# A retention layer's attention core in plain fp32, with the values stationary in four 32-column groups

## The reference

```python
x = L0_attn_x                                  # (4, 1024, 256), fp32
xn = _layernorm(x, axis=-1)
x = x + attn(xn, ...) + ffn(xn, ...)

# attn: 16 heads of 16 channels, no softmax
q, k, v = (xn @ W.T).reshape(b, t, 16, 16)     # W_q, W_k, W_v
decay = where(i >= j, gammas[h] ** (i - j), 0)
attn = einsum('bihd,bjhd->bhij', q, k) * decay / sqrt(16)
y = einsum('bhij,bjhd->bihd', attn, v)
yn = (y - mean) / sqrt(var + EPS)              # over time and channels of each head
out = (yn * gn_weight + gn_bias) @ W_o.T

# ffn: the best 2 of 8 experts for each token
h = relu(xn @ w1[e] + b1[e]);  y_e = h @ w2[e] + b2[e]
out = sum over the two experts of softmax gate * y_e
```

## Time and profile before

| | us |
|---|---|
| median of 3 runs | 861.91 (861.26 to 863.84) |
| the profiled execution | 863.81 |
| its span, first to last instruction | 862.0 |
| TensorE busy in it | 811.3 (94%) |
| VectorE busy | 675.8 (78%) |
| ScalarE busy | 605.8 (70%) |
| GpSimd busy | 416.1 (48%) |

### The profile page before, as it was taken

How to read it: one execution, slowest core, us unless ns; L and a number is a source line. 1 busy time by engine, 2 the same in 40 slices (tenths; PEclk the granted TensorE clock), 3 DMA queues, 4 the chain that set the end, 5 groups by cost and what they waited for, 6 DMA issues and landing times.

```text
span 862.0 us, 21824 instructions
## 1 busy us (share of the span) xinstructions
PE 811.3 (94%) x6976; PEld 775.1 (90%) x6976; DVE 675.8 (78%) x1187; ACT 605.8 (70%) x1073; POOL 416.1 (48%) x352
## 2 busy tenths in 40 slices
PE   3947999999999999989999999999999999999967
PEld 1436999999999999989999999999999999999967
DVE  6687888888888889878778787787877878778646
ACT  2825575767666666767887778877788777887690
POOL 2107777777777677043444434444434443344320
PEclk9977999999999999999999999999999999999998
DMA  9984222222222223758888888878888888888239
GB/s 289 364 308 123 75 82 74 80 73 80 68 82 71 78 71 136 272 182 210 213 244 237 249 220 218 229 236 248 232 202 233 238 246 223 212 238 235 47 76 333
DMA packets 89050, 157.89 MB, mean 183 GB/s; under 512 B 26496, under 2 KB 66560, under 8 KB 78976
## 3 DMA queue, kind: packets, MB, share of 16 engines
q1 hardware_dynamic: 74720, 138.87, 49.1%
q0 software_dynamic: 14304, 18.69, 13.5%
HBM read 111.67 MB, written 37.37 MB: 173 GB/s over the span
## 4 chain that ended last, share of the span: by engine, by line
PE 87%; DVE 5%; issue 3%; DMA 2%; ACT 1%; SPq 1%; POOL 0%; POOLq 0%; DVEq 0%; ACTq 0%
PE ps L662 27%; PE ps L869 26%; PE ps L780 12%; PE ps L718 5%; PE ps L752 3%; PE ps L728 2%; PE ps L926 2%; PE ps L854 2%; PE ps L737 2%; PE ps L680 1%; PE ps L767 1%; DMA xn<-x 1%; PE ps L709 1%; PE ps L804 1%; PE ps L672 1%
## 5 line engine op out<-in xcount | busy, mean ns | idle before, releaser
L662 PE MATMUL ps<-arena_r 128*128 128x256 f32 (+1 forms) x2064 | 262.1, 284 | 0.4 <-ACT xn L561 0.4
L662 PEld LDWEIGHTS ps<-arena_r 128*128 128x128 f32 x2064 | 250.6, 191 | 4.8 <-issue 0.6
L869 PE MATMUL ps<-arena_r 128*128 128x256 f32 x1872 | 232.7, 284 | 0.8 <-DVE gn_t L1287 0.8
L869 PEld LDWEIGHTS ps<-arena_r 128*128 128x128 f32 x1872 | 228.9, 193 | 0.9 <-issue 0.9
L452 POOL TENSOR_TENSOR fence_out<-eps_col 128x1 f32<-128x1 f32 x39 | 78.8, 2020 | 260.3 <-DVE arena_f L1217 260.3
L507 ACT ACTIVATE arena_r<-arena_f 128x2048 fp32r<-128x2048 f32 x78 | 145.5, 1921 | 0.0
L454 POOL DMA_INDIRECT sum_rows<-arena_f,pair_slot x78 | 123.8, 1588 | 18.1 <-issue 17.2
L595 ACT ACTIVATE arena_f<-ps,arena_f 128x256 f32<-128x256 f32 x156 | 65.4, 473 | 90.4 <-PE ps L869 77.8
L780 PE MATMUL ps<-arena_r 128*128 128x128 f32 x1024 | 120.5, 276 | 0.0
L780 PEld LDWEIGHTS ps<-arena_r 128*128 128x128 f32 x1024 | 116.9, 192 | 0.0
L1233 DVE TENSOR_TENSOR arena_r<-arena_f,arena_r 128x2048 fp32r<-128x2048 f32 x39 | 89.4, 2292 | 34.8 <-ACT arena_r L507 34.8
(11 more groups left out here) (143 smaller groups left out, 1103.5 us busy)
## 6 DMA issues: line engine op xcount, KB each, us to landing
arena_f<-w SPq DMA_DIRECT2D x78, 1024.0 KB, 6.1
xs_rows<-spare_rows SPq DMA_DIRECT2D x39, 258.0 KB, 3.7
arena_f<-xs_rows SPq DMA_DIRECT2D x39, 258.0 KB, 3.9
pair_chunk<-xn SPq DMA_DIRECT2D x32, 256.0 KB, 2.5
arena_f<-b SPq DMA_DIRECT2D x39, 128.0 KB, 4.0
xn<-x SPq DMA_DIRECT2D x8, 512.0 KB, 8.9
x_chunk<-xn SPq DMA_DIRECT2D x32, 128.0 KB, 2.0
arena_f<-sum_rows SPq DMA_DIRECT2D x8, 512.0 KB, 7.5
```

Of the source, the lines that this page charges most:

```text
L662: last = pe.matmul(out_ap, lhs(a), rhs(b), start=start and n == 0, stop=stop and n == 2, **kw)
L869: last = pe.matmul(ps[:, 2 + hp, o * SLOT:(o + 1) * SLOT], w1_r[par][:, a, at:at + P], xs_r[:, b, k * SLOT:(k + 1) * SLOT], start=(m == 0 ...
```

## The change

The attention core (scores, state sums, across, inside) drops the split. Scores, keys, queries, values and state stay plain fp32 and go to the matmuls as they are. With that go the high and low parts on ScalarE, VectorE and GpSimd. In `inside` the operands change sides: a head's values (padded to 32 columns with zeros, `v_pad`) are stationary in one of four column groups, and the masked scores stream. The output lies with channels on partitions, so the y transposes and `output_sum` go. Each matmul of `across` has the state stationary and the queries stream, into the same layout. Keys and queries are transposed in separate steps to banks 6 and 5. The scores of a chunk are now issued at the end of the step before. The buffers are placed anew, so that the weights of slot 0 can be loaded ahead of the wait for the scatters; slot 1's wait for the last `inside`.

```diff
-            run_steps(pool, -2, NT, 4, 28, step)
+            run_steps(pool, 0, NT, 4, 28, chunk_scatter)
...
+            sp.wait_ge(s["route_done"], 1)
+            weights_load(0, 0)
+            for par in range(2):
+
+                sp.wait_ge(s[f"scat{par}"], 16 * NT)
+            rows_load(0, 0)
             bias_load(0, 0)
 
-            sp.wait_ge(s["s_l_pool"], NB // 2 * NT)
-            sp.wait_ge(s["s_l_dve"], NB // 2 * NT)
-            slot_load(1, 1)
+            sp.wait_ge(s["y_psum"], NT)
+            weights_load(1, 1)
+            rows_load(1, 1)
...
+            def diagonal_queries(n, par):
+                act.wait_ge(s["qt_psum"], n + 1)
+
+                wait(act, s["s_psum"], NB * (n - 1))
+                for o in range(QH):
+                    nc.scalar.activation(q_diag[:, par, :, o * P:(o + 1) * P], ps[:, 5, D:2 * D].rearrange("p (c i) -> p c i", c=KC),
+                                         ACT.Copy, scale=C["own_head"][:, o:o + 1]).then_inc(s["q_diag"], 1)
...
             def chunk(i, par):
+                if within(i - 1, NT):
+                    output_back(i - 1, 1 - par)
                 if within(i, NT):
+                    queries_back(i, par)
+                if within(i + 1, NT):
+                    values(i + 1, 1 - par)
+                if within(i + 1, NT):
+                    keys_back(i + 1, 1 - par)
+                if within(i + 1, NT):
+                    diagonal_queries(i + 1, 1 - par)
                 if within(i + 2, NT):
+                    tokens_high(i + 2, par)
...
+            run_steps(act, 0, NT, 4, 28, chunk)
+            w_high(0, 0, 0)
+            w_high(1, 0, 0)
+            chunk(NT, NT % 2)
...
             def scores(n, par):
...
                 for c in range(KC):
+                    for g in range(NB):
+                        rows = slice(g * QR, (g + 1) * QR)
...
+                        last = pe.matmul(ps[:, g, c * QH * P:(c + 1) * QH * P], kq_t[rows, par, 0, c * P:(c + 1) * P],
+                                         q_diag[rows, par, c], start=True, stop=True)
...
+            def across(n, par):
...
+                for c in range(KC):
+                    last = pe.matmul(ps[:, 7, c * P:(c + 1) * P], state_f[:, c], kq_t[:, par, 1, c * P:(c + 1) * P],
+                                     start=(c == 0), stop=False, skip_group_check=True)
...
+            def inside(n, par):
...
+                for c in range(KC):
+                    for o in range(QH):
                         for g in range(NB):
+                            h = c * HP + g * QH + o
+                            last = pe.matmul(ps[g * QR:(g + 1) * QR, 7, c * P:(c + 1) * P], v_pad[:, par, h * 2 * DH:(h + 1) * 2 * DH],
+                                             s_f[:, g, (c * QH + o) * P:(c * QH + o + 1) * P], start=False,
+                                             stop=(c == KC - 1 and o == QH - 1), skip_group_check=True)
...
+            def state_sums(n, par):
...
+                    last = pe.matmul(ps[:, 6, 256 + c * P:256 + (c + 1) * P], kq_f[:, par, c * P:(c + 1) * P], v_own(par, c),
+                                     start=(c == 0), stop=(c == KC - 1), skip_group_check=True)
...
             def chunk(i, par):
+                if within(i + 1, NT):
+                    query_projection(i + 1, 1 - par)
+                if within(i + 1, NT):
+                    key_transposes(i + 1, 1 - par)
                 if within(i, NT):
+                    across(i, par)
                 if within(i + 2, NT):
                     x_transposes(i + 2, par)
+                if within(i + 1, NT):
+                    query_transposes(i + 1, 1 - par)
+                if within(i, NT - 1):
+                    state_sums(i, par)
+                if isinstance(i, int) and i == NT - 1:
+                    pe.wait_ge(s["s_f"], NT * NB)
+                    slot_transposes(0, 0)
+                if within(i, NT):
+                    inside(i, par)
+                if within(i + 1, NT):
+                    scores(i + 1, 1 - par)
                 if within(i + 2, NT):
                     key_value_projection(i + 2, par)
...
             def chunk(i, par):
+                if within(i - 2, NT):
+                    output_stats(i - 2)
+                if within(i - 1, NT - 1):
+                    state_sum(i - 1)
+                if within(i + 1, NT):
+                    tokens_low(i + 1, 1 - par)
+                if within(i - 1, NT - 1):
+                    new_state(i - 1)
                 if within(i, NT):
                     masked_scores(i, 0)
                 if within(i, NT):
                     masked_scores(i, 1)
+                if within(i + 1, NT):
+                    keys(i + 1, 1 - par)
                 if within(i, NT):
                     masked_scores(i, 2)
                 if within(i + 1, NT):
+                    queries(i + 1, 1 - par)
                 if within(i, NT):
                     masked_scores(i, 3)
...
+            chunk(NT, NT % 2)
+            chunk(NT + 1, 1 - NT % 2)
             w1_low(0, 0)
             xs_low(0, 0)
```

More of the change, by code:

```diff
@@ L194, in build @@
         rse = ff(NS, E)
+        after_route = ff.at
         ff.at = 0
@@ L705, in x_transposes @@
                 pe.wait_ge(s[f"xc{par}"], (n - par) * 8 + 16)
-                wait(pe, s["v_f"], n)
+                wait(pe, s["v"], n)
                 for k in range(KC):
@@ L730, in query_projection, with slot_transposes @@
                 last.then_inc(s["q_psum"], 1)
-            def kq_transposes(n, par):
-                pe.wait_ge(s["k_f"], n + 1)
+            def slot_transposes(sl, par):
+                pe.wait_ge(s[f"xs_in{par}"], (sl - par) * 8 + 16)
+                wait(pe, s["xst_h"], sl - 1)
+                wait(pe, s["xst_l"], sl - 1)
+                for k in range(KC):
+                    for j in range(SJ):
+                        last = pe.transpose(ps[:, par, (k * SJ + j) * P:(k * SJ + j + 1) * P], xs[:, par, j, k * P:(k + 1) * P], ident)
+                last.then_inc(s["xst_psum"], 1)
@@ L735, in kq_transposes, with key_transposes, query_transposes @@
+            def key_transposes(n, par):
+                pe.wait_ge(s["k_f"], n + 1)
+                wait(pe, s["st_t"], n - 1)
+                for c in range(KC):
+                    last = pe.transpose(ps[:, 6, c * P:(c + 1) * P], kq_f[:, par, c * P:(c + 1) * P], ident)
+                last.then_inc(s["kt_psum"], 1)
+            def query_transposes(n, par):
                 pe.wait_ge(s["q_f"], n + 1)
-                for c in range(2 * KC):
-                    last = pe.transpose(ps[:, 5, c * P:(c + 1) * P], kq_f[:, par, c * P:(c + 1) * P], ident)
@@ L738, in kq_transposes @@
-                last.then_inc(s["kqt_psum"], 1)
+                for c in range(KC):
+                    last = pe.transpose(ps[:, 5, (KC + c) * P:(KC + c + 1) * P], kq_f[:, par, (KC + c) * P:(KC + c + 1) * P], ident)
+                last.then_inc(s["qt_psum"], 1)
             def scores(n, par):
-                pe.wait_ge(s["kqt_h"], n + 1)
-                pe.wait_ge(s["kqt_l"], n + 1)
+                pe.wait_ge(s["k_t"], n + 1)
                 pe.wait_ge(s["q_diag"], QH * (n + 1))
                 for c in range(KC):
-                    for m, (a, b) in enumerate(PASSES):
-                        for g in range(NB):
-                            rows = slice(g * QR, (g + 1) * QR)
-                            if c == 0 and m == 0:
-                                wait(pe, s["s_f"], NB * (n - 1) + g + 1 if not isinstance(n, int) or n > 0 else 0)
-                            last = pe.matmul(ps[:, g, c * QH * P:(c + 1) * QH * P], kq_t[rows, par, 0, a, c * P:(c + 1) * P],
-                                             q_diag[rows, par, b, c], start=(m == 0), stop=(m == 2))
-                            if c == KC - 1 and m == 2:
-                                last.then_inc(s["s_psum"], 1)
@@ L770, in across @@
                 last.then_inc(s["across_done"], 1)
             def inside(n, par):
-                pe.wait_ge(s["s_h"], NB * (n + 1))
-                pe.wait_ge(s["s_l_pool"], 2 * (n + 1))
-                pe.wait_ge(s["s_l_dve"], 2 * (n + 1))
-                for h in range(H):
-                    g, col = h % HP // QH, (h // HP * QH + h % QH) * P
-                    for a in range(2):
-                        last = pe.matmul(ps[:, 7, h // HB * P:(h // HB + 1) * P],
-                                         s_r[:, par, a, g, col:col + P],
-                                         v_wide[:, par, h // HB, h % HB * P:(h % HB + 1) * P], start=False,
-                                         stop=(h == H - 1 and a == 1), skip_group_check=True)
+                pe.wait_ge(s["s_f"], NB * (n + 1))
@@ L837, in _ @@
             for k in range(2):
-                last = pe.matmul(ps[:, 6 + k, 0:NT * E], token_sets[:, k], mask_bf[:], start=True, stop=True)
```

(17 more changed lines are left out.)

297 lines of the change are left out of this document (80 added, 217 removed).

## The result

The changed kernel takes 774.5 us (median), the kernel before 862.9 beside it: a ratio of 0.897, 95% interval 0.894 to 0.900. The profiled execution took 773.2 us with a span of 771.4.

What follows compares the result with a forecast made beforehand. TensorE was taken to bound the attention stage, its chunk falling from 8.66 to 7.5 us: 35 us over 29 periods, plus 3 at the start and 1 at the end, 39 off 861.9, gives 823 us; range 792 to 878.

Steps and rivals of the forecast that it cites:

- The terms that stay: TensorE's chunk work kept: projections and x transposes at 2.29 us, key and query transposes at 0.46.
- The three changes of form: TensorE switching between whole array and row or column groups, three times a chunk at 0.1 us each.
- I take a middle value with a reason: Inside and scores at 1.75 us each: a matmul's two instructions can't overlap, only neighbouring groups' halves do.
- The bounds: Inside and scores each between 0.87 us with groups four abreast and 3.5 us with one at a time.
- Rival 2: Inside and scores four abreast, 0.87 each, chunk 5.7 to 5.9: 774 us; half of it 800; chance 0.17 together.
- the fastest half of case 2: The part of Rival 2 towards full four-abreast packing, 774 us, left out of the range.
- The latency loop: Dependent steps from one chunk's scores to the next, through projections, queries, transposes and diagonal copies: 5.7 us.
- The start: Up to scores of chunk 2, from 87.90 to near 84.5 us: a gain of 3, bounds -2 and +7.
- The feared 4 us for tokens low of chunk 1: At the start, tokens low moves behind VectorE's first chunk, so chunk 1's projection starts some 4 us later.
- The end: Scores of chunk 31 to the first expert layer, 13.2 to 11 us; with layer 2's stall, net gain 1.
- The stall of layer 2: In slot 0, late second weights and their split delay the hidden activations, stalling layer 2 by 1 to 2 us.
- Rival 1: Column groups give no overlap while row groups do: inside 3.5 us, chunk 9.3 with waits, 875 us; chance 0.15.

Runs made afterwards that it cites:

- the one-column run: The changed kernel with all sixteen matmuls of inside writing to the first column group, part of the computation left out: 857.7 us.
- the three kernels with late statistics: Changed kernel with last outputs' statistics behind the low parts, 773.24 us; plus slot 0's hidden activations before slot 1's weights, 771.89; plus early aggregation and moved averaging, 769.35.

## Why the prediction was wrong

- **The direction and what bounds the kernel: right.** TensorE is full before and after, its changed work sets the period, and added work is paid in full (6.87 with 0.87 more).
- **The terms that stay, and plain fp32 on the whole array: near.** Projections and transposes were summed at 2.29 + 0.46 = 2.75 and measure 1.49 + 0.71 + 0.22 + 0.51 = 2.93; across and state sums 0.88 and 0.99, of which 0.10 is the change of form ahead of inside. The three changes of form are 0.1 each, as put: 212 ns between the last start of state sums and the first of inside, where 112 is the step, and much the same behind inside and behind scores. Not foreseen was that the first round in groups is longer, by 0.03 in inside and 0.10 in scores. The 109 ns an instruction from the earlier trace rows came out in inside.
- **"I take a middle value with a reason": the step that failed.** Inside and scores at 1.75 each came from the rule that the two instructions of a matmul block the next group. They measure 1.01 and 1.08, so 1.41 us of the 1.52 by which the period (7.53 with waits) was too long. The other 0.1 is the wait that was allowed and didn't come. The runs show something else in place of the rule: each group takes one running and three waiting instructions, and only a fifth in a row holds the stream. A price near the forecast's does occur, for that other reason, at another order: three matmuls in a row gave 1.74 us and 798 us, four in a row 2.39 and 822.
- **The bounds were right, the choice between them was not.** Both ends, 0.87 and 3.5, stood there; the changed kernel is near the lower one (1.01), and the one-column run at the upper (3.61). Rival 2's 774 is the time measured, and its period of 5.7 to 5.9 is close to the 6.01; that the last microsecond agrees is luck, as its 4 us for the two ends measured 13.6. The rows nearest to the question, four old row groups at 38 ns a matmul, showed nearly full packing, though of matmuls of one instruction each, and the reason that outweighed them came from no row. The range then left out "the fastest half of case 2", the very case.
- **The latency loop: mis-sized, without effect.** The loop was put at 5.7 us with scores at 1.75. With scores at 1.08 that would be 5.0, but the steps measure 5.64: it doesn't go over the query projection (0.71) but over VectorE, whose keys (0.34) and third masked score (0.60 in full) stand ahead of the queries, and from the start of the key-value projection to VectorE's keys it is 1.71, not 1.44. At 6.01 us a chunk it doesn't bound, with about 0.4 us to spare.
- **The start: 3 forecast, 11.2 measured.** Scores of chunk 0 come 2.3 us earlier (62.41), and from there to scores of chunk 2 it is 14.3 us instead of 23.2, two shortened chunks with fewer waits: of TensorE's waits of 3.24, 1.02 and 1.00 us in this stretch one of 0.54 is left. Its clock was at half up to 66.45, from 69.86 to 76.69 and from 83.52 to 86.93 us before, and is now only up to 65.70; the forecast had no term for that. The feared 4 us for tokens low of chunk 1 don't show: they start at 63.88, under the scores of chunk 0.
- **The end: near in its sum.** The 11 us less the 1.41 of inside and scores make 9.6, and 9.3 is measured. The stall of layer 2 was real but hidden, by a cost that was not foreseen: the slow clock behind the gap of 3.9 us, 1.5 us. That the moved weight load is worth nothing on its own, the run with the late load showed.
- **Rival 1's premise was fair, its price high.** With no column overlap the kernel takes 858, not 875, as scores do overlap: a gain of 5, not a loss.

Left open: that the waits on registers' values, read one after another, are what loosens scores in the rolled loop is an inference from four starts and from the unrolled chunks beside them; no run changed them alone. Nor is it shown why they stay tight when TensorE doesn't wait. Open too is how deep a row group's queue is beyond four.

## What to carry to other kernels

Small matmuls in the four 32-row or 32-column groups run four abreast even when each is two instructions (here 1.01 us where one group alone takes 3.61), as long as the program puts at most four instructions of one group in a row; the loop over the groups innermost does that. When a cost has two bounds far apart and nothing but a mechanism of your own between them, put the range over both ends, and weigh the rows that show packing above the mechanism. And when the bounding engine gets a third lighter, write out the latency loop of the stage with every step on it: here it was 0.4 us behind, and once TensorE had to wait, only 0.06.

## What the runs showed of the hardware

- Four column groups take 32 fp32 instructions of 128 columns in 1.01 us, against 3.61 in one group. Starts within a round are 6 to 7 ns apart for inside and for scores; with two matmuls of a group in a row they are mostly 13 to 14 ns apart in either.
- With eight instructions of a column group in a row, TensorE starts matmuls of different groups out of the order of the program (196.221 ahead of 196.324), if the starts are put to groups by their spacing.
- With six or eight instructions of a group in a row, the next group's first starts 6 ns behind the fourth from last; with four in a row all groups run side by side.
- Each change between the whole array, column groups and row groups costs some 0.1 us: 212 ns instead of 112 ahead of inside, 222 instead of 109 between inside and scores. The first round is longer too, 134 ns instead of 109 in inside, and 320 instead of 216 in scores.
- TensorE idle for 3.9 us at the full clock was followed by 3.4 us at 1.2 GHz (260.26 to 263.67). With the gap at 1.8 us layer 1 ran at 2.4 GHz in the three kernels with late statistics, and at 1.2 GHz until 262.50 in a second profiled execution of the last of them.
